# A ring of ten tiles, an inversion spread over 7.3 chains, back steps two chains later, and every fourth message pair split in halves

## The chip, the cores and the metric

One Trainium2 chip, one core, one launch. The metric is the device time of the kernel in microseconds (us), the median of some runs. The engines are TensorE (PE; PEld is its weight load), VectorE (DVE), ScalarE (ACT), GpSimd (POOL) and SyncE (SP, which here issues DMAs only). Each runs its own instructions in order, and semaphores tie them together.

## The reference, cut to what matters

The kernel computes two layers of a graph network on 2048 tokens of width 512. The change touches two of its stages.

The first is the gated delta recurrence of the first layer. Every token goes to 2 of 4 experts, so there are 4096 slots; the kernel works on them as 32 tiles of 128 slots, 8 heads of 64.

```python
def step(S, x):
    qt, kt, vt, bt, gt = x
    S = S * jnp.exp(gt)[..., None, None]
    kv = jnp.einsum('bhk,ebhkv->ebhv', kt, S)
    delta = (vt[None] - kv) * bt[..., None]
    S = S + kt[None, :, :, :, None] * delta[..., None, :]
    ot = jnp.einsum('bhk,ebhkv->ebhv', qt * scale, S)
    return (S, ot)
```

The second is the message passing of the second layer, over 32768 edges:

```python
msg = jax.nn.relu(x[src] + edge_attr @ W_e + b_e)
aggr = jax.ops.segment_sum(msg, dst, num_segments=x.shape[0])
```

## The kernel before, in words

Each stage is written as a `plan`, a list of (time, what, number) that is sorted by time. Every engine walks the list and issues what is its own, so the plan's times fix the order on each engine and nothing else; semaphores do the waiting. The unit of the plan's times is one chain in the recurrence and one pair of edge blocks in the message stage.

**The recurrence (tiles named `delta_...`).** A tile's 8 heads are worked in two chains of four heads, so there are NC = 64 chains. A chain has a front, which needs no state: GpSimd's mask (L1931) and ScalarE's part of it, transposes of q and k (L2068, copied by ScalarE), the decay sums on TensorE (L2080 to L2082, the last two in fp32r, one pass), their exp, GpSimd's weighting (L1936), the gram matmuls (L2093), and on VectorE the key products `BA` (L2194). `BA` and the transposed `kq` stand in a ring of R = 9 tiles; one part of `kq` lies in `X`.

The recurrence inside a tile asks for the inverse of a unit triangular matrix of 128 x 128 per head. Its diagonal blocks of 32 x 32 are inverted on VectorE for a batch of four tiles (eight chains) at once: SP writes the blocks to memory ("B out"), loads them as `Bs` with one block per partition ("B in", L1868), VectorE sets `Us` to minus `Bs` times a strict mask, with ones on the diagonal ("blocks set", L2169 and L2172), and walks 30 columns, each a product into `tmp` (L2176) and an update of `Us` (L2179). ScalarE copies the transpose to `Ls` (L1957), SP writes both out (L1871, L1873) and loads them in another layout for each tile ("UL in", L1883 and L1887). The rest of the inversion is small matmuls: Z (L2101, L2103), U (L2111 to L2115), Zb and T (L2043, L2050).

A chain's back carries the state: "through" (L2129), then on VectorE `r` and the first half of `o` (L2202, L2209), "solve" (L2138), `w` on ScalarE, "sums" (L2146 and L2151), then `state` (L2219) and `o` (L2225) on VectorE, and SP stores `o`. `kd` is GpSimd's weighted key (L1945). MAIN = 17.2 is the plan's distance from a chain's front to its back, MID = 15.8 that to Z; a batch's columns stand 5.4 chains wide in the plan behind 8 (q + 1) + 0.75 (3.0 chains wide for the first batch). With the backs run the products of a gate ("gate"), for which the stage's last chains have room.

**The message stage (tiles named `conv_...`).** The edges are sorted by target; 144 pairs of blocks of 128 edges are worked. Per pair: GpSimd gathers two blocks of source rows (L2702), TensorE transposes the attributes (L2717) and multiplies them by `W_e` into two banks (L2722), VectorE adds the gathered rows (L2768), ScalarE applies relu in place (L2749), TensorE sums by target with a one-hot matrix `hot` (L2730), and VectorE adds the bank to the accumulator (L2779). VectorE makes `hot` by comparison (L2760), for two pairs at a time. All of it is f32.

The planned times of the columns before are these:

```python
at = 0.75 + (5.4 if q else 3.0) * (31 - k) / 31
part = at - int(at)
part = part + 0.5 if part < 0.18 else 0.76 + 0.66 * (part - 0.18)
plan.append((first + int(at) + part, "block column", (q, k)))
```

## Time and profile before

| | us |
|---|---|
| median of 3 runs | 3208.61 (3206.28 to 3215.51) |
| the profiled execution, its own time | 3215.7 |
| its span | 3213.9 |
| TensorE busy | 2905.2 (90%) |
| VectorE busy | 1669.4 (52%) |
| GpSimd busy | 1488.0 (46%) |
| ScalarE busy | 1136.8 (35%) |
| mean granted clock of TensorE | 0.959 of full speed |

The busy shares are means over some twenty stages with different limits. What a stage is worth is read from windows of the trace that hold that stage alone: the recurrence lies at 1343 to 1948 us, the message stage at 2330 to 2777 us.

### The profile page before, as it was taken

The page shows a single profiled execution, that of the slowest core. Times are in us where ns is not written, and L with a number is a line of the kernel's source. Part 1 is how long each engine was busy: PE and PEld are TensorE (multiplying, and loading weights), DVE is VectorE, ACT ScalarE, POOL GpSimd, SP SyncE. Part 2 cuts the span into 40 slices and gives each one's busy share as a digit, 9 for nine tenths or more (in the row PEclk, how much of TensorE's full clock was granted, in tenths as well). Part 3 has the DMA queues.
Part 4 walks back from the last instruction along what each step waited for, and adds up shares of the span by engine and source line. Part 5 has one row for each costly group of instructions (what it writes and reads, how often), then busy time and mean ns, then how long its engine had stood idle before and what let it go on. Part 6 is the DMA issues. An engine that isn't in the chain of part 4 may idle for free.

```text
span 3213.9 us, 46196 instructions
## 1 busy us (share of the span) xinstructions
PE 2905.2 (90%) x16081; PEld 1658.6 (52%) x16081; DVE 1669.4 (52%) x3820; ACT 1136.8 (35%) x2501; POOL 1488.0 (46%) x1471
## 2 busy tenths in 40 slices
PE   6999999988899899858989898999999999999828
PEld 3433566667676644447777664444533333444424
DVE  7633355578344432268777643442267777521361
ACT  3312422289122222346666441220044444331201
POOL 0565756488654537633333204545566666200004
PEclk9999999999999999979999998999999999999959
DMA  5400001120111234434454454211176666500404
GB/s 173 140 19 5 7 25 49 46 71 16 32 52 44 72 121 165 166 104 126 117 143 128 136 148 159 77 53 38 49 227 199 198 205 190 156 0 27 183 0 132
DMA packets 275961, 321.38 MB, mean 100 GB/s; under 512 B 155807, under 2 KB 193569, under 8 KB 275732
## 3 DMA queue, kind: packets, MB, share of 16 engines
q1 hardware_dynamic: 219684, 182.57, 18.7%
q0 software_dynamic: 51840, 134.60, 13.4%
q8 instruction: 132, 2.16, 0.3%
q10 hardware_dynamic: 4208, 1.25, 0.2%
...
## 4 chain that ended last, share of the span: by engine, by line
PE 74%; issue 10%; DVE 5%; ACT 4%; POOL 4%; DMA 2%; SPq 0%; ACTq 0%; POOLq 0%; DVEq 0%
PE bank L2730 8%; PE bank L1522 5%; PE bank L2722 5%; PE bank L708 4%; PE bank L1301 4%; PE bank L2393 3%; PE bank L2884 3%; PE bank L2877 3%; PE bank L439 3%; PE bank L731 2%; PE bank L762 2%; PE bank L1117 2%; PE bank L2373 2%; PE bank L1311 2%; PE bank L858 2%
## 5 line engine op out<-in xcount | busy, mean ns | idle before, releaser
L2702 POOL DMA_INDIRECT conv_src<-xn_rows,keep x288 | 272.9, 948 | 175.7 <-DVE conv_msg L2768 110.4
L291 POOL DMA_INDIRECT sorted_bias<-perf_rec,place x256 | 259.7, 1014 | 146.0 <-PE bank L708 91.6
L2730 PE MATMUL bank<-conv_msg,conv_hot 128*128 128x512 f32 x576 | 273.0, 596 | 0.6 <-ACT conv_msg L2749 0.6
L2768 DVE TENSOR_TENSOR conv_msg<-bank,conv_src 128x512 f32<-128x512 f32 x288 | 185.5, 686 | 47.2 <-PE bank L2722 47.2
L1936 POOL TENSOR_TENSOR delta_dec<-delta_dec,rates_of 128x512 f32<-128x512 f32 x64 | 68.8, 1075 | 282.5 <-ACT delta_dec L1988 282.5
L666 POOL DMA_INDIRECT sorted_edge<-rec,place x128 | 127.1, 993 | 141.4 <-PE bank L1362 75.0
L2749 ACT ACTIVATE conv_msg<-conv_msg 128x1024 f32<-128x1024 f32 x144 | 152.0, 1056 | 102.0 <-DVE conv_msg L2768 102.0
L1117 PE MATMUL bank<-bias_prod,bias_hot 128*128 128x256 f32 x640 | 148.2, 387 | 25.1 <-ACT bias_hot L1070 13.0
L2722 PE MATMUL bank<-conv_we,conv_eT 64*128 64x512 f32 x576 | 164.5, 648 | 0.7 <-ACT conv_eT L2746 0.7
L1101 POOL TENSOR_TENSOR bias_prod<-bias_col,bias_rec 128x512 f32<-128x512 f32 x128 | 147.2, 1179 | 16.4 <-PE bank L1117 15.7
L1117 PEld LDWEIGHTS bank<-bias_prod,bias_hot 128*128 128x128 f32 x640 | 120.1, 192 | 53.7 <-issue 28.1
L2730 PEld LDWEIGHTS bank<-conv_msg,conv_hot 128*128 128x128 f32 x576 | 106.7, 205 | 71.5 <-issue 69.4
L2779 DVE TENSOR_TENSOR acc<-acc,bank 128x512 f32 x144 | 99.0, 688 | 72.6 <-PE bank L2730 72.6
L2194 DVE TENSOR_TENSOR delta_BA<-bank,delta_dec 128x512 f32<-128x512 f32 x128 | 82.1, 682 | 99.8 <-issue 51.3
L439 PE MATMUL bank<-xnT,perf_w 128*128 128x512 f32 x256 | 117.0, 600 | 3.5 <-ACT xnT L470 2.1
L3048 POOL TENSOR_TENSOR mlp_mv<-mlp_mv,neg_half 128x1 f32<-128x1 f32 x12 | 6.6, 552 | 242.3 <-DVE mlp_mv L3015 242.3
L889 ACT ACTIVATE mix_ex<-bank,mix_t 128x266 f32<-128x266 f32 x128 | 54.8, 479 | 159.9 <-DVE mix_t L947 159.9
L2884 PE MATMUL bank<-mlp_h,keep 128*128 128x512 f32 x256 | 110.5, 592 | 0.0
L2877 PE MATMUL bank<-mlp_hT,mlp_w 128*128 128x512 f32 x256 | 110.4, 592 | 0.0
L1079 ACT ACTIVATE bias_far<-C,bias_rec 128x128 f32<-128x128 f32 x320 | 102.2, 390 | 20.9 <-DMA bias_rec<-sorted_bias 14.2
L2138 PE MATMUL bank<-delta_r,delta_U 128*128 128x128 f32 (+1 forms) x512 | 71.7, 286 | 38.6 <-DVE delta_o L2209 32.1
L2722 PEld LDWEIGHTS bank<-conv_we,conv_eT 64*128 64x128 f32 x576 | 43.8, 186 | 109.7 <-issue 108.4
...
## 6 DMA issues: line engine op xcount, KB each, us to landing
...
conv_src<-xn_rows,keep POOLq DMA_INDIRECT x288, 3.6
...
sorted_bias<-perf_rec,place POOLq DMA_INDIRECT x256
```

Of the source, the lines that this page charges most:

```text
L291: POOL.indirect_dma_start(out=sorted_bias, out_offset=bass.IndirectOffsetOnAxis(ap=place[:, 0, c:c + 1], axis=0), in_=rec0[:, c, :], in_of ...
L439: a = PE.matmul(bank[i % 2], w[:, side, c, m * P:(m + 1) * P], xnT[:, c, nb * 512:(nb + 1) * 512], start=c == 0, stop=c == KC - 1)
L1101: engine.tensor_tensor(prod[:, q:q + 2, :, :], col[:, g % 2, k:k + 2, :].unsqueeze(2).broadcast_to([P, 2, H, GW]), rec[:, g % 3, k:k + 2, ...
L1117: a = PE.matmul(bank[u % 8][:, 0:W], hot[:, i // PER % 2, i % PER + j, :], prod[:, i % 8 + j, :, :].rearrange("p h j -> p (h j)"), start=j ...
L1522: a = PE.matmul(bank[3 + n % BANKS], xnT[:, c, t * P:(t + 1) * P], wts[k][:, c, :], start=c == 0, stop=c == KC - 1)
L2702: POOL.indirect_dma_start(out=src[:, n % 4, j, :], out_offset=None, in_=xn_rows, in_offset=bass.IndirectOffsetOnAxis(ap=rec[:, g % 3, k + ...
L2722: a = PE.matmul(bank[2 + 2 * q + j][:, :], eT[half, q, :], we[half, :], start=True, stop=True)
L2730: a = PE.matmul(bank[n % 2][:, :], hot[:, g % 2, k + j, :], msg[:, q, j, :], start=j == 0, stop=j == 1)
L2749: ACT.activation(msg[:, q, :, :], msg[:, q, :, :], AF.Relu).then_inc(*active.up())
L2768: DVE.tensor_tensor(msg[:, q, j, :], bank[2 + 2 * q + j][:, :], src[:, n % 4, j, :], ALU.add).then_inc(*raw.up())
L2877: a = PE.matmul(bank[i % 4], w1[:, c, m * P:(m + 1) * P], hT[:, c, columns(nb)], start=c == 0, stop=c == KC - 1)
L2884: return PE.matmul(bank[4 + nb], w2[:, c, m * P:(m + 1) * P], h1[:, c, columns(nb)], start=c == 0, stop=c == 2 * KC - 1)
```

## The change

In the recurrence the ring `BA` and `kq` have ten tiles instead of nine, and all steps of the backs and the middle of the inversion stand two chains later in the plan. To make room, `kd`, `r` and `w` have one copy instead of two, `o` three instead of four and `kv` two instead of three, with the waits that this asks for. The strict mask is left out of the set. The columns of a batch stand over 7.3 chains instead of 5.4 (from the second batch on), and a column is two entries of the plan: a product and an update; where a product falls ahead of the key products, its update stands behind them.

In the message stage every pair n with n % 4 == 1 is split: ScalarE writes relu of the message as `high` in fp32r, VectorE computes relu of the message less `high` as `low` in fp32r, and the scatter takes four fp32r matmuls instead of two f32 ones. `hot` is written as fp32r (its values are 0 and 1) and read as f32 by the other pairs. The two additions of gathered rows become one of double length, and the steps ahead of the sum stand up to 0.75 of a pair's time earlier.

```diff
...
-            R = 9
+            R = 10
             BT = 4
             NBT = ST // BT
             NC = 2 * ST
-            MID, MAIN = 15.8, 17.2
-            ALONE, TWO, FIRST = 16, 14, 16
+            MID, MAIN = 17.8, 19.2
+            ALONE, TWO, FIRST = 18, 16, 18
...
-            kv = sb("kv", [P, 3, 2, D])
+            kv = sb("kv", [P, 2, 2, D])
...
-            kd, r_, w = (sb(n, [P, 2, HG, HD]) for n in ("kd", "r", "w"))
-            o = sb("o", [P, 4, HG, HD])
+            kd, r_, w = (sb(n, [P, HG, HD]) for n in ("kd", "r", "w"))
+            o = sb("o", [P, 3, HG, HD])
...
-                plan.append((2 * t + (14.6 if t >= 2 else 13.6 + 0.4 * t), "UL in", t))
-                plan.append((2 * t + MAIN - 3.0, "load kv", t))
+                plan.append((2 * t + (16.6 if t >= 2 else 13.6 + 0.4 * t), "UL in", t))
+                plan.append((2 * t + MAIN - 2.6, "load kv", t))
...
-                    at = 0.75 + (5.4 if q else 3.0) * (31 - k) / 31
+                    at = 0.75 + (7.3 if q else 3.0) * (31 - k) / 31
                     part = at - int(at)
                     part = part + 0.5 if part < 0.18 else 0.76 + 0.66 * (part - 0.18)
-                    plan.append((first + int(at) + part, "block column", (q, k)))
-                plan.append((first + (6.33 if q else 5.19), "L copy", q))
-                plan.append((first + (6.34 if q else 5.2), "blocks out", q))
+                    plan.append((first + int(at) + part, "block product", (q, k)))
+                    plan.append((first + int(at) + (0.745 if q and part < 0.7 else part), "block update", (q, k)))
+                plan.append((first + (8.23 if q else 5.19), "L copy", q))
+                plan.append((first + (8.24 if q else 5.2), "blocks out", q))
...
                     if what == "load kv":
-                        if n >= 3:
-                            SP.wait_ge(*kd_ready.at(2 * (n - 3) + 2))
-                            SP.wait_ge(*r_ready.at(2 * (n - 3) + 2))
-                        SP.dma_start(kv[:, n % 3, :, :], slot_qkv[n * P:(n + 1) * P, D:3 * D].rearrange("p (a d) -> p a d", a=2)
-                                     ).then_inc(*kv_in[n % 3].up(16))
+                        if n >= 2:
+                            SP.wait_ge(*kd_ready.at(2 * (n - 2) + 2))
+                            SP.wait_ge(*r_ready.at(2 * (n - 2) + 2))
+                        SP.dma_start(kv[:, n % 2, :, :], slot_qkv[n * P:(n + 1) * P, D:3 * D].rearrange("p (a d) -> p a d", a=2)
+                                     ).then_inc(*kv_in[n % 2].up(16))
...
+                        if n >= 1:
+                            POOL.wait_ge(*state_sum.at(n))
+                        POOL.tensor_tensor(kd[:, :, :], kv[:, t % 2, 0, g * W:(g + 1) * W].rearrange("p (h d) -> p h d", d=HD),
                                            mid(bg[:, t, hs], HD), ALU.mult).then_inc(*kd_ready.up())
...
                     if what == "w":
                         ACT.wait_ge(*solved.at(n + 1))
-                        ACT.activation(flat4(w[:, n % 2, :, :]), MA[:, 256:512], AF.Copy, scale=-1.0).then_inc(*w_ready.up())
+                        if n >= 1:
+                            ACT.wait_ge(*attended.at(n))
+                        ACT.activation(flat4(w[:, :, :]), MA[:, 256:512], AF.Copy, scale=-1.0).then_inc(*w_ready.up())
...
                     if what == "blocks set":
                         DVE.wait_ge(*bs_in.at(16 * (n + 1)))
-                        if n == 0:
-                            DVE.wait_ge(*strict_in.at(16))
                         if n >= 1:
                             DVE.wait_ge(*u_out.at(16 * n))
                             DVE.wait_ge(*L_ready.at(n))
-                        DVE.scalar_tensor_tensor(flat(Us), flat(Bs), -1.0, strict[:, :], ALU.mult, ALU.mult
-                                                 ).then_inc(*blocks.up())
+                        DVE.tensor_scalar(flat(Us), flat(Bs), -1.0, None, ALU.mult).then_inc(*blocks.up())
                         DVE.wait_ge(*blocks.now())
                         DVE.memset(flat(Us)[:, 0:32 * 32:33], 1.0).then_inc(*blocks.up())
-                    if what == "block column":
+                    if what == "block product":
                         q, k = n
                         DVE.wait_ge(*blocks.now())
                         DVE.tensor_tensor(tmp[:, 0:k, k + 1:32], Bs[:, 0:k, k:k + 1].broadcast_to([P, k, 31 - k]),
                                           Us[:, k:k + 1, k + 1:32].broadcast_to([P, k, 31 - k]), ALU.mult).then_inc(*blocks.up())
+                    if what == "block update":
+                        q, k = n
                         DVE.wait_ge(*blocks.now())
                         a = DVE.tensor_tensor(Us[:, 0:k, k + 1:32], Us[:, 0:k, k + 1:32], tmp[:, 0:k, k + 1:32], ALU.subtract)
                         if k > 1:
...
                     if what == "r":
                         DVE.wait_ge(*through.at(n + 1))
-                        DVE.wait_ge(*kv_in[t % 3].at(16 * (t // 3 + 1)))
+                        DVE.wait_ge(*kv_in[t % 2].at(16 * (t // 2 + 1)))
+                        if n >= 1:
+                            DVE.wait_ge(*solved.at(n))
                         for i, h in enumerate(heads):
-                            a = DVE.scalar_tensor_tensor(r_[:, n % 2, i, :], (MA, MB)[i % 2][:, (i // 2) * HD:(i // 2 + 1) * HD],
-                                                         eg[:, 0, t, h:h + 1], kv[:, t % 3, 1, h * HD:(h + 1) * HD],
+                            a = DVE.scalar_tensor_tensor(r_[:, i, :], (MA, MB)[i % 2][:, (i // 2) * HD:(i // 2 + 1) * HD],
+                                                         eg[:, 0, t, h:h + 1], kv[:, t % 2, 1, h * HD:(h + 1) * HD],
                                                          ALU.mult, ALU.subtract)
                         a.then_inc(*r_ready.up())
-                        if n >= 4:
-                            DVE.wait_ge(*o_out[n % 4].at(16 * (n // 4)))
+                        if n >= 3:
+                            DVE.wait_ge(*o_out[n % 3].at(16 * (n // 3)))
...
-            hot = sb("hot", [P, 2, PER, P])
+            hot = sb("hot", [P, 2, PER, P], F32H)
...
+            high, low = (sb(n, [P, 2, 2, D], F32H) for n in ("high", "low"))
...
+
+            def in_halves(n):
+
+                return n % 4 == 1
 
             plan = []
             for n in range(EG):
-                for what, at in (("gather", -3.6), ("turn", -2.3), ("eT", -2.2), ("edge", -1.75), ("raw", -1.4), ("relu", -0.85),
+                for what, at in (("gather", -3.9), ("turn", -3.05), ("eT", -2.9), ("edge", -2.15), ("raw", -1.8), ("relu", -1.25),
                                  ("sum", 0.0), ("add", 0.6)):
                     plan.append((n + at, what, n))
+                if in_halves(n):
+                    plan.append((n - 0.7, "low", n))
                 if n % 2 == 0:
                     plan.append((n - 2.2, "hot", n // 2))
...
                         PE.wait_ge(*prepared.at(2 * n // SOME + 1))
                         if n >= 2:
                             PE.wait_ge(*added.at(n - 1))
+                        if not in_halves(n):
+                            for j in range(2):
+                                a = PE.matmul(bank[n % 2][:, :], hot[:, g % 2, k + j, :].bitcast(F32), msg[:, q, j, :],
+                                              start=j == 0, stop=j == 1)
+                            a.then_inc(*summed.up())
+                            continue
                         for j in range(2):
-                            a = PE.matmul(bank[n % 2][:, :], hot[:, g % 2, k + j, :], msg[:, q, j, :], start=j == 0, stop=j == 1)
+                            PE.matmul(bank[n % 2][:, :], hot[:, g % 2, k + j, :], high[:, n // 4 % 2, j, :], start=j == 0, stop=False)
+                        PE.wait_ge(*lowered.at(n // 4 + 1))
+                        for j in range(2):
+                            a = PE.matmul(bank[n % 2][:, :], hot[:, g % 2, k + j, :], low[:, n // 4 % 2, j, :], start=False,
+                                          stop=j == 1)
                         a.then_inc(*summed.up())
...
                     if what == "relu":
-                        ACT.wait_ge(*raw.at(2 * n + 2))
-                        ACT.activation(msg[:, q, :, :], msg[:, q, :, :], AF.Relu).then_inc(*active.up())
+                        ACT.wait_ge(*raw.at(n + 1))
+                        if not in_halves(n):
+                            ACT.activation(msg[:, q, :, :], msg[:, q, :, :], AF.Relu).then_inc(*active.up())
+                            continue
+                        if n >= 8:
+                            ACT.wait_ge(*summed.at(n - 7))
+                        ACT.activation(high[:, n // 4 % 2, :, :], msg[:, q, :, :], AF.Relu).then_inc(*active.up())
...
-                        for j in range(2):
-                            DVE.tensor_tensor(msg[:, q, j, :], bank[2 + 2 * q + j][:, :], src[:, n % 4, j, :],
-                                              ALU.add).then_inc(*raw.up())
+                        DVE.tensor_tensor(msg[:, q, :, :], pairs[1 + q][:, :, :], src[:, n % 4, :, :], ALU.add).then_inc(*raw.up())
+                    if what == "low":
+                        DVE.wait_ge(*active.at(n + 1))
+                        if n >= 8:
+                            DVE.wait_ge(*summed.at(n - 7))
+                        DVE.scalar_tensor_tensor(low[:, n // 4 % 2, :, :], msg[:, q, :, :], 0.0, high[:, n // 4 % 2, :, :].bitcast(F32),
+                                                 ALU.max, ALU.subtract).then_inc(*lowered.up())
```

**VectorE in the recurrence, one chain in the middle of a batch.** First before, then the change (`delta_tmp` rows are products, `delta_Us` rows updates, `delta_BA` the key products).

```order
L2202 SCALAR_TENSOR_TENSOR delta_r<-bank,delta_eg,delta_kv 128x64 x4
L2209 TENSOR_TENSOR delta_o<-bank,delta_eg 128x2x64 x2
L2176 TENSOR_TENSOR delta_tmp<-delta_Bs,delta_Us 128x18x13
L2179 TENSOR_TENSOR delta_Us<-delta_Us,delta_tmp 128x18x13
L2194 TENSOR_TENSOR delta_BA<-bank,delta_dec 128x2x256 x2
L2176 TENSOR_TENSOR delta_tmp<-delta_Bs,delta_Us 128x17x14
L2179 TENSOR_TENSOR delta_Us<-delta_Us,delta_tmp 128x17x14
L2176 TENSOR_TENSOR delta_tmp<-delta_Bs,delta_Us 128x16x15
L2179 TENSOR_TENSOR delta_Us<-delta_Us,delta_tmp 128x16x15
L2219 SCALAR_TENSOR_TENSOR delta_state<-delta_state,delta_ep,bank 128x64 x2
L2176 TENSOR_TENSOR delta_tmp<-delta_Bs,delta_Us 128x15x16
L2179 TENSOR_TENSOR delta_Us<-delta_Us,delta_tmp 128x15x16
```

```order
L2202 SCALAR_TENSOR_TENSOR delta_r<-bank,delta_eg,delta_kv 128x64 x4
L2209 TENSOR_TENSOR delta_o<-bank,delta_eg 128x2x64 x2
L2172 TENSOR_TENSOR delta_tmp<-delta_Bs,delta_Us 128x21x10
L2192 TENSOR_TENSOR delta_BA<-bank,delta_dec 128x2x256 x2
L2177 TENSOR_TENSOR delta_Us<-delta_Us,delta_tmp 128x21x10
L2172 TENSOR_TENSOR delta_tmp<-delta_Bs,delta_Us 128x20x11
L2177 TENSOR_TENSOR delta_Us<-delta_Us,delta_tmp 128x20x11
L2219 SCALAR_TENSOR_TENSOR delta_state<-delta_state,delta_ep,bank 128x64 x2
L2172 TENSOR_TENSOR delta_tmp<-delta_Bs,delta_Us 128x19x12
L2177 TENSOR_TENSOR delta_Us<-delta_Us,delta_tmp 128x19x12
L2225 TENSOR_TENSOR delta_o<-delta_o,bank 128x256
```

Between the first half of `o` and the state there were three pairs of product and update, one of them ahead of the key products; now there are two, and of the first only the product stands ahead of the key products.

**SP in the recurrence, from the end of one batch's inversion to the load of the next.** First before, then the change.

```order
L1871 DMA sol_u<-delta_Us 128x1024
L1873 DMA sol_l<-delta_Ls 128x1024
L1883 DMA delta_U<-sol_u 32x8x32 x4
L1887 DMA delta_Lf<-sol_l 32x8x32 x3
L1850 DMA keep<-slot_qkv 128x1024
L1910 DMA slot_out<-delta_o 128x256
L1862 DMA sol_b<-delta_BA 32x8x32 x4
L1910 DMA slot_out<-delta_o 128x256
L1856 DMA delta_kv<-slot_qkv 128x1024
L1868 DMA delta_Bs<-sol_b 128x1024
```

```order
L1868 DMA sol_u<-delta_Us 128x1024
L1870 DMA sol_l<-delta_Ls 128x1024
L1865 DMA delta_Bs<-sol_b 128x1024
L1880 DMA delta_U<-sol_u 32x8x32 x4
L1884 DMA delta_Lf<-sol_l 32x8x32 x3
```

The load of `Bs` stood behind two stores and a batch of "B out"; now it is the next DMA after the writes of the finished batch, since these have moved two chains later and it has not.

**TensorE in the message stage, two pairs of which the first is a split one.** First before, then the change.

```order
L2730 MATMUL bank<-conv_msg,conv_hot 128x512 x2
L2722 MATMUL bank<-conv_we,conv_eT 128x512 x2
L2717 MATMUL bank<-C,conv_att 128x128
L2730 MATMUL bank<-conv_msg,conv_hot 128x512 x2
L2722 MATMUL bank<-conv_we,conv_eT 128x512 x2
L2717 MATMUL bank<-C,conv_att 128x128
```

```order
L2742 MATMUL bank<-conv_high,conv_hot 128x512 x2
L2745 MATMUL bank<-conv_low,conv_hot 128x512 x2
L2728 MATMUL bank<-conv_we,conv_eT 128x512 x2
L2723 MATMUL bank<-C,conv_att 128x128
L2737 MATMUL bank<-conv_msg,conv_hot 128x512 x2
L2728 MATMUL bank<-conv_we,conv_eT 128x512 x2
L2723 MATMUL bank<-C,conv_att 128x128
```

The two f32 matmuls of the split pair have become two with `high` and two with `low`; the rest of the pair stands where it stood.

## Rows read from the trace of the kernel before

**Rows 1.** Windows of four stages: us, busy time of each engine, PEclk, DMA share, GB/s.
```profile
1343.00:1437.00 94.00, 56.92 (x386) 38.19 (x386) 50.82 (x107) 45.28 (x118) 37.34 (x36) 0.80 0.32 95
1437.00:1812.00 375.00, 339.71 (x5114) 280.11 (x5114) 285.61 (x874) 238.29 (x650) 124.27 (x138) 0.97 0.47 126
1812.00:1948.00 136.00, 120.86 (x1658) 90.41 (x1657) 58.58 (x220) 47.49 (x140) 11.39 (x18) 0.91 0.49 143
2330.00:2777.00 447.00, 441.75 (x1296) 151.49 (x1296) 326.97 (x503) 207.37 (x306) 272.93 (x288) 0.99 0.67 197
```

**Rows 2.** Chain of waits, message stage: start, us, what, count.
```profile
2399.57 1.72 PE bank L2730 x4
...
2402.61 1.72 PE bank L2730 x4
```

**Rows 3.** Timeline of TensorE, recurrence, a decay sum.
```profile
1562.54 0.59 PE L2081 MATMUL bank<-delta_dec_half,delta_after_half 128*128 128x512 f32 x1
1562.97 0.40 PE L2082 MATMUL bank<-delta_dec_half,delta_after_half 128*128 128x512 f32 x1
```

**Rows 4.** VectorE groups of the message stage: count, busy us, mean ns, idle before.
```profile
L2768 DVE TENSOR_TENSOR conv_msg<-bank,conv_src 128x512 f32<-128x512 f32 x288 | 185.5, 686 | 47.2 <-PE bank L2722 47.2
L2779 DVE TENSOR_TENSOR acc<-acc,bank 128x512 f32 x143 | 98.3, 688 | 70.8 <-PE bank L2730 70.8
```

**Rows 5.** Timelines of GpSimd and of VectorE, message stage.
```profile
2506.70 0.95 POOL L2702 DMA_INDIRECT conv_src<-xn_rows,keep  x1 [0.30 <-issue]
...
2506.89 0.68 DVE L2760 TENSOR_TENSOR conv_hot<-C,keep 128x512 f32<-128x512 f32 x1
```

**Rows 6.** Timeline of VectorE, recurrence, chains with inversion columns.
```profile
1504.78 0.41 DVE L2225 TENSOR_TENSOR delta_o<-delta_o,bank 128x256 f32<-128x256 f32 x1
...
1516.56 1.12 DVE L2179 TENSOR_TENSOR delta_Us<-delta_Us,delta_tmp 128x234 f32<-128x234 f32 x1
...
1521.80 0.41 DVE L2225 TENSOR_TENSOR delta_o<-delta_o,bank 128x256 f32<-128x256 f32 x1
```

**Rows 7.** Timeline of VectorE, chains without columns, then the next set.
```profile
1543.77 1.29 DVE L2194 TENSOR_TENSOR delta_BA<-bank,delta_dec 128x512 f32<-128x512 f32 x2 [2.74 <-issue]
...
1550.83 1.29 DVE L2194 TENSOR_TENSOR delta_BA<-bank,delta_dec 128x512 f32<-128x512 f32 x2 [2.99 <-issue]
...
1560.53 1.23 DVE L2169 SCALAR_TENSOR_TENSOR delta_Us<-delta_Bs,delta_strict 128x1024 f32<-128x1024 f32 x1 [0.40 <-DMA delta_Bs<-sol_b]
```

**Rows 8.** Waits, middle part of the recurrence: total, times, longest us.
```profile
PE bank L2138 <- DVE delta_o L2209: 31.5, 32, 2.0
```

**Rows 9.** Window of one batch of eight chains, columns as in rows 1.
```profile
1497.00:1560.00 63.00, 56.47 (x876) 46.36 (x876) 49.34 (x150) 40.43 (x111) 21.65 (x24) 1.00 0.50 133
```

**Rows 10.** VectorE groups, middle part, inversion columns.
```profile
L2179 DVE TENSOR_TENSOR delta_Us<-delta_Us,delta_tmp 128x58 f32<-128x58 f32 (+4 forms) x179 | 74.3, 415 | 6.1
L2176 DVE TENSOR_TENSOR delta_tmp<-delta_Bs,delta_Us 128x58 f32<-128x58 f32 (+4 forms) x179 | 68.5, 382 | 2.4
```

**Rows 11.** Timeline of SP's DMA queue, end of a batch and next load.
```profile
1539.89 0.32 SPq L1871 DMA_DIRECT2D sol_u<-delta_Us  x1
1542.11 0.32 SPq L1873 DMA_DIRECT2D sol_l<-delta_Ls  x1
...
1555.80 0.32 SPq L1868 DMA_DIRECT2D delta_Bs<-sol_b  x1
```

**Rows 12.** Timeline of TensorE, lead-in, fronts alone.
```profile
1356.79 0.38 PE L2080 MATMUL bank<-delta_mask_bits 128*128 128x512 bf16 x1 [0.88 <-issue]
...
1360.00 0.38 PE L2080 MATMUL bank<-delta_mask_bits 128*128 128x512 bf16 x1 [0.88 <-issue]
```

**Rows 13.** Timeline of VectorE, tail, one row per chain.
```profile
1923.86 0.42 DVE L2225 TENSOR_TENSOR delta_o<-delta_o,bank 128x256 f32<-128x256 f32 x1 [0.55 <-PE bank L2151]
...
1947.01 0.42 DVE L2225 TENSOR_TENSOR delta_o<-delta_o,bank 128x256 f32<-128x256 f32 x1 [1.42 <-PE bank L2151]
```

**Rows 14.** Window of the last chains, columns as in rows 1.
```profile
1925.00:1948.00 23.00, 18.73 (x201) 16.56 (x200) 6.44 (x27) 5.07 (x15) 0.61 (x1) 0.70 0.33 99
```

35 lines of the change are left out of this document (14 added, 21 removed).

## The prediction

> **What bounds the kernel now.** I read the stage windows first [rows 1], to see how much of each stage TensorE is busy; then, inside the two stages that the diff touches, the chain of waits, the grouped instructions and the timelines.
>
> In the message stage TensorE is busy 442 of 447 us and every other engine has room (VectorE 327, GpSimd 273) [rows 1]. The chain of waits there is TensorE alone, and it repeats every 2402.61 - 2399.57 = 3.04 us, one pair of edge blocks; 1.72 of them are the scatter matmuls [rows 2]. What is taken from these comes off the span.
>
> The recurrence has three parts: fronts alone (94 us), both together (375 us), backs alone (136 us) [rows 1]. In the middle part a chain (half a tile) without inversion columns takes 1550.83 - 1543.77 = 7.1 us, and VectorE waits 2.7 and 3.0 us in it before its key products: TensorE sets the pace [rows 7]. With columns, two chains take 1521.80 - 1504.78 = 17.0, 8.5 each [rows 6], and over the middle part TensorE stands 31.5 us in 32 waits before the solve because VectorE has not finished r and the first half of o [rows 8]. So some 5.4 chains of every 8 go at VectorE's pace and the rest at TensorE's.
>
> **The change, part by part.**
>
> Message stage. Every fourth pair, 36 of 144, replaces two f32 scatter matmuls by four in fp32r (high and low part of the message). The trace has fp32r matmuls of 128x512 in the decay sums: L2081 ends at 1562.54 + 0.59 = 1563.13, L2082 at 1562.97 + 0.40 = 1563.37, so one takes 0.24 us, its weight load included [rows 3]. Four take 0.96 against 1.72: 0.76 x 36 = 27 us off the chain. Bounds: 31 if each is an even quarter of the f32 matmul that it stands for (1.72/8 = 0.215), 18 if every third halved pair loses its gain to a wait.
>
> Is there a new wait? Four pairs will take TensorE 4 x 3.04 - 0.76 = 11.4 us. VectorE has in them eight message additions (or four of double length, at most 8 x 0.69), four scatter additions (0.69) [rows 4], two comparisons (0.68) [rows 5] and now one subtraction on 128x1024; the nearest row, the set in the recurrence, took 1.23 us [rows 7]: 10.9 us at most. The subtraction stands 0.7 of a pair's time ahead of the matmuls that need it, and the high part's matmuls go first. GpSimd issues two gathers per pair, each 0.95 us and 0.30 between them [rows 5]: 10.0 of 11.4 us. ScalarE only writes its result elsewhere. I take no wait; the cover is thin (0.5 us on VectorE), and each microsecond that it falls short in four pairs costs 36 us.
>
> A lock between VectorE and GpSimd would speak against this. In the trace a comparison with two inputs in SBUF ran from 2506.89 to 2507.57 while a gather was issued, and both kept their usual 0.68 and 0.95 us [rows 5]. The Trainium skill ("SBUF — State Buffer", the section on a bandwidth-pool intuition that is wrong) says that while VectorE runs an operation over both ports GpSimd cannot write the descriptors of its own DMAs. By that rule the new subtraction would add its length to GpSimd's queue, which would then need 11.2 of 11.4 us and still not be the bound.
>
> Inversion over 7.3 chains. VectorE is busy 49.3 of the 63 us of a batch of eight chains [rows 9]. Its work for the chains themselves: in the middle part 285.6 us [rows 1], less 74.3 + 68.5 for columns [rows 10] and five sets of 1.23 [rows 7], leaves 137 us over 46 chains, 3.0 each. A batch's inversion is then 49.3 - 8 x 3.0 = 25 us. Over 5.4 chains that is 4.7 + 3.0 = 7.7 us a chain, above TensorE's 7.1; over 7.3 chains it is 3.5 + 3.0 = 6.5, below it. Measured against load, the slow chains took (63 - 2.6 x 7.1)/5.4 = 8.25 for 7.7, 7% more; 6.5 with that is 7.0. At best the batch falls to 8 x 7.1 = 56.8, 6.2 us less. But the peak is thicker than the mean: an update takes 1.12 us instead of 0.42 when a GpSimd operation runs beside it [rows 6, 10]. From below I take a quarter of the best, 1.5 us. I take 4, two thirds of the best, because the order still puts one or two pairs ahead of r. The update that is held back until after the key products changes no work; it lets TensorE's next gram matmuls start some 0.4 us sooner, inside the 4.
>
> The set of the next batch. Its mask falls away: 1.23 us [rows 7] becomes a scaling with one input. No row has this form at this size; it lies between the 1.23 and the 0.68 of a 128x512 operation [rows 5], and I take 0.9, 0.3 less. Against it, there is now one chain, not three, between the last column and the set. SP must write U, wait for ScalarE's copy, write L (2.2 us after U), then load Bs; that load took 1560.53 - 1555.80 = 4.7 us [rows 7, 11]. That is 7.3 us for a chain of 7.1, where the wait was 0.4 [rows 7]: 0 to 1.5 us more, also inside the 4.
>
> The ring of ten and the two chains' delay. No work is added or removed: two chains leave the middle part, and two fronts and two backs run alone. The middle part is now 375/46 = 8.15 us a chain; then 44 x (8.15 - 0.5) = 337, so -38 us. Lead-in: a front alone takes 1360.00 - 1356.79 = 3.2 us [rows 12], so +6.4 at most; r of the first chain no longer stands behind the second batch's set, so 3 at least; I take +5. Tail: its last three backs took 1947.01 - 1923.86 = 23.2, 7.7 us each [rows 13], at a mean granted clock of 0.70, between the levels 1.2 and 2.4 GHz [rows 14]; two more cost 15 (14 at 7.1, 17 at 8.5). Sum: -38 + 5 + 15 = -18 us.
>
> The single copies of kd, r and w, three of o and two of kv add waits on work that ends most of a chain earlier (the sums, solve or attention of the chain before; for kv 2.3 chains, against a load the size of Bs's 4.7 us), so nothing. Behind SP's wait for r before it loads kv stand the store of o and the loads of U and L, whose slack is 1.1 chains.
>
> Sum: -27 - 18 = -45 us. The profiled execution took 3215.7 us about a span of 3213.9, 7 above the median of 3208.6. From the median: **3164 us**; its profile nearer 3171.
>
> **The rivals.**
> 1. The chains gain little: VectorE's waits move to the set, one after each batch, and the columns before r still keep the solve waiting. For it: the gap of 7.1 us against 7.3. Against it: a load of 6.5 us. At 1.5 us a batch the middle part gives -16 - 8 = -24, the recurrence -4, the kernel -31: 3178.
> 2. The message stage stops being TensorE's, VectorE being late with the low part or the additions. For it: 10.9 of 11.4 us; against it: that is an upper bound. Half the gain goes: -13 - 18 = -31: 3178.
> 3. The whole excess goes (56.8 a batch): 44 x 0.78 = 34, with -16 and +20 it is -30; the kernel -57: 3152.
> 4. Slower: the tables come too late. U is written at once after the last column, L 2.2 us later [rows 11], then both are read back in small loads; the first Z of a batch stands 1.5 chains, 10.8 us, behind the last column, and stood 1.4 behind it. If each of seven batches waited there for x us, the kernel would be slower from 7x > 45, x > 6.4. At 8 us: 3220. Against it: the distance grew.
> 5. TensorE's clock is granted less: it is 0.97 in the middle part, 0.80 in the lead-in [rows 1], 0.70 at the end [rows 14]. Two more thin chains at each end at the lower level cost +10 to +20 beyond the sum; with rival 1, about 3195.
> On the last, the Trainium skill ("TensorE: Matmul & The Clock Gate", Part 1) says that the clock is low by default and that activity releases it; the trace agrees, with 0.99 in its fullest stage and less at the thin ends. By the rule the longer ends stay partly at the lower level, which is case 5.
>
> **How the numbers follow.** The sum as argued 0.60; rival 1 0.15; rival 2 0.08; rival 3 0.08; rival 4 0.04; rival 5 0.05. The range takes in rivals 1 to 3 with the bounds of the matmul: 3147 (rival 3 with 31 for the messages, and a microsecond) to 3187 (rival 1 with 18 for the messages). A measurement here tells 0.3%, 10 us, from no change. Faster 0.91 (the first four cases), same 0.05, slower 0.04.
>
> **What the profile will show.** Message stage: four fp32r matmuls within 1.0 us, four pairs in 11.4 us, the stage some 27 us shorter, no wait of TensorE for the low part. Recurrence: chains with columns 7.3 to 7.6 us instead of 8.5, TensorE's wait before the solve far under 31.5 us, 0 to 2 us of wait at each set, the first solve 3 to 6 us later after the first decay, a tail near 151 us. Wrong would be: chains that stay above 8 us, sets that wait over 3 us, Z waiting for the L load in each batch, or gathers longer than 0.95 us beside the subtraction.

## The result, and the profile after

The changed kernel took 3185.97 us (median of 5 runs, 3181.11 to 3194.41) against 3208.82 (5 runs, 3206.28 to 3215.51) of the kernel before, taken together: ratio 0.9929, interval 0.9911 to 0.9947, 22.8 us faster. The forecast was 45 faster, 3164; the range held the time, at its upper end. The same kernel was measured twice more (below): 0.9967 (0.9951 to 0.9982) on a chip where before took 3253 us, and 0.9904 (0.9886 to 0.9921) on one where it took 3212.

The profiled execution had a span of 3179.3 us, its own time 3181.1, the fastest of its five; that of before was the slowest of its five. The difference of the two profiles, 34.6 us, is therefore more than the medians give.

Windows of the changed kernel, the stages of [rows 1] at their new places, then one batch of eight chains [rows 9]; columns as there:

```profile
1343.00:1450.00 107.00, 65.65 (x436) 45.03 (x438) 57.33 (x128) 50.02 (x131) 40.73 (x41) 0.78 0.32 90
1450.00:1788.00 338.00, 314.60 (x4876) 257.32 (x4874) 253.14 (x828) 226.23 (x620) 114.40 (x132) 1.00 0.48 131
1788.00:1930.00 142.00, 127.48 (x1855) 97.43 (x1853) 63.28 (x245) 54.55 (x157) 12.65 (x20) 0.95 0.52 152
2313.00:2742.00 429.00, 414.54 (x1296) 151.76 (x1296) 346.20 (x396) 209.28 (x306) 290.45 (x288) 0.99 0.70 205
1492.00:1553.60 61.60, 57.34 (x892) 46.86 (x892) 45.49 (x150) 41.37 (x114) 21.00 (x24) 1.00 0.50 134
```

Two things stand out beside [rows 1]. In the message stage TensorE is now 14 us short of always busy, where it lacked 5. And the middle of the recurrence has clock 1.00, where it had 0.97.

**Message stage: a wait nobody had before.** Chain of waits of the changed kernel in this stage (start, us, what):

```profile
2455.45 0.02 ACT conv_msg L2766
...
2456.42 1.05 ACT conv_att L2756
2457.47 0.04 issue
2457.51 0.33 PE bank L2723
2457.84 0.47 PE bank L2742 x2
2458.32 0.46 PE bank L2745 x2
2458.78 1.06 PE bank L2728 x4
2459.84 0.26 PE bank L2723
2460.10 1.72 PE bank L2737 x4
```

The four fp32r matmuls (L2742, L2745) take 0.47 + 0.46 = 0.93 us where 1.72 stood, as forecast. But once in eight pairs the chain leaves TensorE and runs over ScalarE's pack, the copy of the next eight pairs of edge rows into `att` (L2756, 1.05 us). Timeline of ScalarE and TensorE at another such place (in brackets the idle time before, and who ended it):

```profile
2408.75 1.06 ACT L2766 ACTIVATE conv_msg<-conv_msg 128x1024 f32<-128x1024 f32 x1 [0.96 <-DVE conv_msg L2788]
...
2409.71 1.04 ACT L2756 ACTIVATE conv_att<-keep 128x1024 f32<-128x1024 f32 x1
2410.80 0.14 PEld L2723 LDWEIGHTS bank<-C,conv_att 128*128 128x128 f32 x1 [1.38 <-ACT conv_att L2756]
2410.81 0.33 PE L2723 MATMUL bank<-C,conv_att 128*128 128x128 f32 x1 [0.55 <-ACT conv_att L2756]
```

The plan has the pack at n - 3.0, as before, while the change moved the turn that reads it from n - 2.3 to n - 3.05. The pack, queued behind a relu, now ends after the turn is due. From one turn to the next it is 3.04 us for an ordinary pair, 2.25 for a split one and 3.66 at these places; from the first turn to the last 417.4 us against 435.9 before.

**Recurrence: three terms, two of them off.** From the timelines, the first output of a chain (L2225) came at 1441.1 before and 1453.7 after, the last decay sum at 1810.5 and 1786.6, the last output at 1947.0 and 1929.3 (the changed kernel's times are put 0.14 us later, so that the first decay sums, 1343.21 and 1343.07, meet). So the lead-in is +12.6 us (forecast +5), the middle 369.4 to 332.9, -36.5 (-38), the tail 136.5 to 142.7, +6.2 (+15). Their sum is -17.7 for -18, which is chance: the lead-in lost what the tail saved, and part of the middle's gain is not what I had argued.

VectorE of the changed kernel in the middle, two chains with columns:

```profile
1563.98 0.30 DVE L2172 TENSOR_TENSOR delta_tmp<-delta_Bs,delta_Us 128x150 f32<-128x150 f32 x1
1565.95 1.29 DVE L2192 TENSOR_TENSOR delta_BA<-bank,delta_dec 128x512 f32<-128x512 f32 x2 [1.68 <-issue]
1567.16 0.44 DVE L2177 TENSOR_TENSOR delta_Us<-delta_Us,delta_tmp 128x150 f32<-128x150 f32 x1
...
1570.41 0.85 DVE L2202 SCALAR_TENSOR_TENSOR delta_r<-bank,delta_eg,delta_kv 128x64 f32<-128x64 f32 x4
...
1573.23 1.29 DVE L2192 TENSOR_TENSOR delta_BA<-bank,delta_dec 128x512 f32<-128x512 f32 x2 [1.28 <-issue]
```

From key products to key products it is 7.3 us here, from output to output 7.1 to 8.4 over a batch, where a chain with columns took 8.5 [rows 6]; the batch is 61.6 us for 63.2 to 63.8. VectorE idles 1.3 to 1.7 us ahead of the key products and then has no gap until r; the held-back update stands in that full stretch. TensorE's wait for VectorE before the solve fell to half [rows 8], not to nearly nothing, and the set waits little. The second row is new, a wait for ScalarE (below):

```profile
PE bank L2137 <- DVE delta_o L2209: 15.5, 26, 1.4
PE bank L2137 <- ACT delta_U L2002: 7.1, 5, 1.4
```

```profile
1554.24 0.69 DVE L2166 TENSOR_SCALAR delta_Us<-delta_Bs 128x1024 f32<-128x1024 f32 x1 [0.84 <-DMA delta_Bs<-sol_b]
```

**Recurrence: another wait nobody had before.** Once in each batch, at the first solve behind the end of the columns, TensorE stands 1.4 us for ScalarE's copy of the finished inverse (`U`, L2005 before, L2002 after). ScalarE before, then ScalarE and TensorE of the changed kernel:

```profile
1539.80 0.38 ACT L2005 ACTIVATE delta_U<-bank 64x256 f32<-64x256 f32 x1
1540.08 2.00 ACT L1957 ACTIVATE delta_Ls<-delta_Us 128x1024 f32<-128x1024 f32 x1
```

```profile
1546.77 1.98 ACT L1954 ACTIVATE delta_Ls<-delta_Us 128x1024 f32<-128x1024 f32 x1
1548.78 0.38 ACT L1999 ACTIVATE delta_Zb<-bank 64x256 f32<-64x256 f32 x1
1549.18 0.38 ACT L2002 ACTIVATE delta_U<-bank 64x256 f32<-64x256 f32 x1
1549.61 1.10 PE L2137 MATMUL bank<-delta_r,delta_U 128*128 128x128 f32 x8 [1.44 <-ACT delta_U L2002]
```

The 2 us copy of the transpose (`L copy`) stood behind the two small copies (Zb and T) and now stands ahead of them. In the plan those two lie at 0.25 and 0.26 of a chain's time; the change moved the L copy from 6.33 to 8.23 behind a batch's start, from just behind them to just ahead. In the four profiles with the spread of 5.4 the L copy stands behind the small ones, in the ten with 7.3 ahead of them; all ten have this wait, five times each, and none of the four has it in the middle. VectorE's r and first half of `o` were done at 1547.5 and TensorE's last decay sum at 1548.2, so the solve could have started 1.4 us sooner. No run moved the L copy back; that it would give up to 1.4 us a batch, 7 us in five, is an estimate from these rows.

In the lead-in VectorE of the changed kernel stands at the second batch's set, and the key products of chain 17 are queued behind it; TensorE then idles for those key products, ahead of its next gram matmuls:

```profile
1424.30 1.29 DVE L2192 TENSOR_TENSOR delta_BA<-bank,delta_dec 128x512 f32<-128x512 f32 x2 [1.93 <-POOL delta_dec L1933]
1431.84 0.69 DVE L2166 TENSOR_SCALAR delta_Us<-delta_Bs 128x1024 f32<-128x1024 f32 x1 [6.25 <-DMA delta_Bs<-sol_b]
...
1433.12 1.28 DVE L2192 TENSOR_TENSOR delta_BA<-bank,delta_dec 128x512 f32<-128x512 f32 x2
```

```profile
1434.55 2.08 PE L2092 MATMUL bank<-delta_more_kq 64*128 64x256 f32 x8 [3.78 <-DVE delta_BA L2192]
```

### The profile page after: what moved, and what is told of

Same layout as the page of the kernel before. It is cut to its first block, busy times and chain, and to the rows that moved or that the text cites. A ratio compares the mean times of both kernels' runs of the same rounds, so it can differ in the third digit from the quotient of the medians.

```text
span 3179.3 us, 46211 instructions
## 1 busy us (share of the span) xinstructions
PE 2868.6 (90%) x16081; PEld 1650.9 (52%) x16081; DVE 1667.8 (52%) x3712; ACT 1138.0 (36%) x2501; POOL 1497.0 (47%) x1471
## 4 chain that ended last, share of the span: by engine, by line
PE 80%; DVE 7%; ACT 6%; issue 5%; DMA 2%; POOL 1%; SPq 0%; DVEq 0%; ACTq 0%; POOLq 0%
PE bank L1522 5%; PE bank L2737 5%; PE bank L708 4%; PE bank L2728 4%; PE bank L1301 4%; PE bank L2393 3%; PE bank L2909 3%; PE bank L2902 3%; PE bank L439 3%; PE bank L2137 2%; PE bank L731 2%; PE bank L2150 2%; PE bank L762 2%; PE bank L1117 2%; PE bank L2128 2%
## 5 line engine op out<-in xcount | busy, mean ns | idle before, releaser
L2708 POOL DMA_INDIRECT conv_src<-xn_rows,keep x288 | 290.4, 1009 | 140.8 <-issue 95.9
L2737 PE MATMUL bank<-conv_msg,conv_hot 128*128 128x512 f32 x432 | 203.5, 594 | 0.0
L2788 DVE TENSOR_TENSOR conv_msg<-bank,conv_src 128x1024 f32<-128x1024 f32 x144 | 175.7, 1220 | 18.0 <-PE bank L2728 18.0
L2766 ACT ACTIVATE conv_msg<-conv_msg 128x1024 f32<-128x1024 f32 x108 | 114.2, 1057 | 87.3 <-DVE conv_msg L2788 87.3
L2909 PE MATMUL bank<-mlp_h,keep 128*128 128x512 f32 x256 | 110.5, 592 | 0.0
L2737 PEld LDWEIGHTS bank<-conv_msg,conv_hot 128*128 128x128 f32 x432 | 80.1, 205 | 52.4 <-issue 51.8
L1942 POOL TENSOR_TENSOR delta_kd<-delta_kv,delta_bg 128x256 f32<-128x256 f32 x64 | 39.2, 613 | 130.4 <-PE bank L2145 129.9
```

The lines of the kernel that those rows point to most:

```text
L2708: POOL.indirect_dma_start(out=src[:, n % 4, j, :], out_offset=None, in_=xn_rows, in_offset=bass.IndirectOffsetOnAxis(ap=rec[:, g % 3, k + ...
L2737: a = PE.matmul(bank[n % 2][:, :], hot[:, g % 2, k + j, :].bitcast(F32), msg[:, q, j, :], start=j == 0, stop=j == 1)
L2788: DVE.tensor_tensor(msg[:, q, :, :], pairs[1 + q][:, :, :], src[:, n % 4, :, :], ALU.add).then_inc(*raw.up())
L2909: return PE.matmul(bank[4 + nb], w2[:, c, m * P:(m + 1) * P], h1[:, c, columns(nb)], start=c == 0, stop=c == 2 * KC - 1)
```

## The experiments

Each time stands beside runs of the kernel before on the same chip. The two halves, the early pack and the update at once shared a chip (before 3214.0 us); the second measurement of the change, the spread of 5.4, the earlier load and the two pairs another (3253.2); all four together, every second pair split and 5.4 with the update at once a third (3212.7); the third measurement of the change stood on a fourth (3211.7). The microseconds faster or slower are worked out from the ratio; the difference of the two medians lies up to 3 us beside them.

**The two halves apart.** The kernel before with the changed message stage, and the changed kernel with the old message stage.

> The kernel before, with the change's message stage and with its recurrence left as it was. In the changed kernel's profile the turns of the message stage take 417.4 us from first to last against 435.9 before. Theory (the stage gives its 18 us wherever it stands): ratio near 0.994, 17 to 20 us faster than before; the pattern 3.04 us for a pair, 2.25 for a split one and 3.66 for one in each eight is found again. Rival (the message stage gave its forecast 27 us, and the recurrence then gave nothing or cost in the median): 25 to 29 us faster, ratio 0.991 to 0.992.

Measured: 3195.92 us, ratio 0.9949 (0.9933 to 0.9965), 16.4 us faster; turns 417.4 us from first to last, the same pattern. The stage gives what its own profile shows.

> The changed kernel with the message stage of before. Its profile ended the recurrence 17.7 us sooner than the profile of before, but that execution of before was its slowest, with dips of the granted clock in the recurrence that cost it about 10 us. Theory (the recurrence itself gives only some 5 to 8 us, and the dips made the rest): 3 to 9 us faster than before in the median, ratio 0.997 to 0.999. Rival (the profiles' 17.7 us are the recurrence's): ratio near 0.9945.

Measured: 3200.35 us, 0.9962 (0.9944 to 0.9981), 12.2 us faster: between the two theories, with an interval (6 to 18) that reaches both. Its profile has the changed kernel's batches of 61.6 us to a few hundredths. 16.4 + 12.2 = 28.6.

The third measurement of the whole change was to say whether the halves add.

> The changed kernel a third time. Its first measurement gave 22.8 us less than before, the second, on a chip where the kernel of before took 3253 us, 10.7 less; the two halves of the change measured apart gave 16.4 and 12.2, 28.6 in all. Theory (the halves add): 25 to 31 us faster than before on a chip where before takes 3205 to 3215 us. Rival (together they give less than apart): 18 to 23 us.

Measured: 3183.50 us, 0.9904, 30.8 us faster. That the halves add fits this, within the 6 us either way that its interval leaves; the first 22.8 and this 30.8 are two measurements of one kernel, so differences of 8 us between kernels on different chips say little.

**The pack.** One number:

```diff
-                    plan.append((n - 3.0, "pack", n // HALF))
+                    plan.append((n - 3.5, "pack", n // HALF))
```

> The changed kernel with ScalarE's packing of the next eight pairs of edge rows half a pair sooner in the order (n - 3.5 in place of n - 3.0), so that it no longer stands right ahead of the copy that frees the turn, and behind a relu. Theory (the one long period in each eight pairs, 3.66 us for 3.04, is the turn waiting for the pack): the long periods go, 17 times 0.62 us, 9 to 11 us faster than the changed kernel, 32 to 34 faster than before (ratio 0.9895 to 0.990). Rival 1 (the stage is near VectorE's 10.9 us in 11.4 for four pairs and takes the freed time as waits for the raw sums or the low parts): 2 to 6 us. Rival 2 (the pack then delays a relu by its 1.05 us and moves the wait to the sums): 0 us.

Measured: 3174.09 us, 0.9875 (0.9858 to 0.9892), 40.2 us faster than before. Beside the changed kernel's 22.8 and 30.8 that is 9 to 17 more; the stage itself is exact, 407.4 us from first turn to last for 417.4. Its timeline:

```profile
2405.83 1.05 ACT L2756 ACTIVATE conv_att<-keep 128x1024 f32<-128x1024 f32 x1
2406.90 1.06 ACT L2766 ACTIVATE conv_msg<-conv_msg 128x1024 f32<-128x1024 f32 x1
...
2408.33 0.33 PE L2723 MATMUL bank<-C,conv_att 128*128 128x128 f32 x1
```

The turn has no wait, eight pairs take 22.73 us, and 435.9 - 407.4 = 28.5 us is the forecast's 27 with the one wait removed. Both rivals fall.

**How far the split goes.** Also with the early pack, every second pair split (`return n % 2 == 1`, the halves' buffers and waits to match).

> The changed kernel with the pack half a pair sooner and every second pair split in halves instead of every fourth. By the rows of the changed kernel four pairs then cost PE 2 x 3.04 + 2 x 2.25 = 10.6 us, and VectorE 4 x (1.22 merged sum + 0.69 addition + 0.34 hot) + 2 x 1.22 low = 11.4 us, before waits. Theory (at every fourth pair VectorE was just under PE, the next one passes it): 11.4 to 12 us for four pairs, no faster than the 11.36 with every fourth pair split, 0 to 20 us slower than the kernel with the pack alone moved. Rival (VectorE's sums overlap and PE stays the bound): 10.6 us for four pairs, stage 27 us shorter.

Measured: 3195.28 us, 0.9945 (0.9924 to 0.9966); 425.4 us from first turn to last, 11.9 for four pairs against 11.4, though undisturbed stretches of eight pairs took 21.2, the rival's 10.6 for four. So it is slower, as the theory said, but not by the mechanism it named. VectorE's work is 310 of 350 us, and TensorE waits 25.8 of them for the low part; the engine that is full is GpSimd. Groups of GpSimd in 350 us (2350 to 2700) of before, of the changed kernel, with the early pack, and with every second pair split (count, busy us, mean ns, idle before):

```profile
L2702 POOL DMA_INDIRECT conv_src<-xn_rows,keep x231 | 218.9, 947 | 132.3 <-DVE conv_msg L2768 92.8 <-issue 39.4
```

```profile
L2708 POOL DMA_INDIRECT conv_src<-xn_rows,keep x241 | 242.7, 1007 | 108.6 <-issue 68.5 <-DVE conv_msg L2788 40.1
```

```profile
L2708 POOL DMA_INDIRECT conv_src<-xn_rows,keep x247 | 275.5, 1116 | 76.2 <-issue 69.5 <-DVE conv_msg L2788 6.7
```

```profile
L2708 POOL DMA_INDIRECT conv_src<-xn_rows,keep x235 | 277.1, 1179 | 73.6 <-issue 69.3 <-DVE conv_msg L2788 4.2
```

With its fixed 0.30 us between gathers (235 x 0.30 = 70 us) it is busy 347 of 350 us, and 2 x (1.18 + 0.30) = 2.96 us a pair is 11.8 of the 11.9 us for four. A gather grows when one of VectorE's operations with both inputs in SBUF, the subtraction or the comparison, runs beside it. In the 350 us with the early pack the 153 gathers beside neither took 0.94 to 0.96 us, the 62 beside a comparison alone 1.19 in the mean and the 31 beside a subtraction 1.78. In the kernel with every second pair split:

```profile
2490.05 1.21 DVE L2793 SCALAR_TENSOR_TENSOR conv_low<-conv_msg,conv_high 128x1024 fp32r<-128x1024 f32 x1
2490.12 1.96 POOL L2708 DMA_INDIRECT conv_src<-xn_rows,keep  x1 [0.30 <-issue]
```

1.96 us for 0.95: 1.01 more, beside 1.14 us of the subtraction. The Trainium skill ("SBUF — State Buffer", the section on the bandwidth-pool intuition) tells of such a wait of GpSimd, which cannot write its descriptors until VectorE lets go of the shared port, but for a `tensor_copy`, with one input; the trace has it for operations with two inputs. By these sums it decides here how far the split can go: with the early pack GpSimd is as full (275.5 + 247 x 0.30 = 350 us), and TensorE too. Shares between a fourth and a half of the pairs, and an order that keeps VectorE's two operations off the gathers, were not tried.

**The inversion's spread and the held-back update.**

```diff
-                    plan.append((first + int(at) + (0.745 if q and part < 0.7 else part), "block update", (q, k)))
+                    plan.append((first + int(at) + part, "block update", (q, k)))
```

> The changed kernel with each key-product block's update right behind its product again, not held back to 0.745 of its chain; the spread over 7.3 chains stays. The profile shows VectorE idle 1.2 to 1.9 us ahead of the key products in each chain with columns, while the held update (0.44 to 0.70 us) stands behind them and ahead of the right side r. Theory (the held order costs in the middle of the recurrence): 30 to 40 chains by 0.3 to 0.5 us, 9 to 20 us faster than the changed kernel. Rival (without the hold the pair stands between the state and the key products, on VectorE's other tight path, as in the kernel before): equal or 5 to 15 us slower.

Measured: 3182.77 us, 0.9906 (0.9891 to 0.9921). A batch took 60.7 to 61.1 us for 61.6, so holding the updates back cost, but 0.8 us a batch where I expected 1.5 to 3; by the last decay sum it was 4 us ahead of the changed kernel, counted from the first one, and the tail (147.7 us for 142.7, its last 30 us at clock 0.78 for 1.00) gave that back. The time is not told apart from the changed kernel's.

Next, the spread alone undone, with and without the hold (`5.4 if q` for `7.3 if q`, the copy of L and the writes at their old 6.33 and 6.34).

> The changed kernel with the inversion of a batch spread over 5.4 chains as before (L copy and blocks out back at 6.33 and 6.34), all else of the change kept: ring of ten, back steps two chains later, set with one operand, updates held back. Theory (the spread is what shortens a batch, and the other parts are even): a batch of eight goes back from 61.6 to 63.5 to 64 us, six batches, 10 to 13 us slower than the changed kernel. Rival (the lighter set and the ring give the gain, the spread nothing): 61 to 62 us a batch, within 3 us of the changed kernel.

Measured: 3276.55 us, 1.0078 (1.0050 to 1.0106) where the unaltered changed kernel on the same chip had 0.9967: 36 us slower than it, three times the theory's price. Its batches took 64.8 to 67.8 us; of the 39 us between the two profiles 30 lie in the recurrence behind its first output. It says that the change depends on the spread, not what the spread alone is worth, since the clock fell in every batch (below).

> The changed kernel with the inversion spread over 5.4 chains and each update right behind its product: of the recurrence's change only the ring of ten, the back steps two chains later and the one-operand set are left. With the updates held back and 5.4 chains an undisturbed batch of eight took 64.8 us, before 63.5 to 63.8. Theory (the held updates made the 1.3 us, and ring, set and later back steps are even in the middle): 63.2 to 64.2 us where the clock stays up. Rival (the later back steps themselves lengthen the chains): 64.5 us or more. Both expect falls of the granted clock again, of 2 to 4 us each, in the stretches where VectorE is busy without a gap and PE waits.

Measured: 3198.09 us, 0.9956 (0.9940 to 0.9973). Of the five batches from the first output on, four took 63.2 to 63.4 us and one 66.2, with a fall of the clock. So ring, later back steps and light set are even in the middle, as forecast, and the 14 us that this kernel is faster than before are no more than the message stage's 16.4. With updates at once, 7.3 chains for 5.4 are worth 63.4 - 60.8 = 2.6 us a batch, the new wait for ScalarE (1.4 us, only with 7.3) already paid, and holding back takes 0.8 of them again. With 5.4 chains it does more harm: TensorE's longest wait for the solve is 3.4 us, where it is 1.9 with updates at once.

**The clock is the rest.** Windows of the kernel before around its longest wait for the solve (columns as in rows 1), and that wait in TensorE's timeline, with another one a batch later:

```profile
1586.00:1588.00 2.00, 0.47 (x3) 0.04 (x1) 1.93 (x8) 0.60 (x1) 0.81 (x1) 1.00 0.60 182
1590.00:1598.00 8.00, 8.00 (x95) 6.98 (x95) 7.26 (x24) 4.10 (x13) 0.00 (x0) 0.50 0.50 114
```

```profile
1588.47 1.22 PE L2138 MATMUL bank<-delta_r,delta_U 128*128 128x128 f32 x8 [2.00 <-DVE delta_o L2209]
...
1682.55 0.21 PE L2101 MATMUL bank<-delta_Lf,delta_BA 32*32 32x32 f32 x1 [1.61 <-DMA delta_Lf<-sol_l]
```

TensorE stood 2.00 us behind VectorE, and 1.61 for the load of L, and then, from about 1 and 2 us later, ran for some 10 and 7 us at 0.50 of the clock, 1.2 GHz for 2.4: those two batches took 67.2 and 67.8 us, the others 63.2 to 63.8. The message-alone kernel, whose recurrence is the old one, has two such batches (67.2 and 67.6), behind waits of 1.90 and 1.28 us, and one with a fall of some 3 us behind a wait of 1.88 that took 63.7 like the rest. Not every such wait is followed by a fall, so its length alone does not decide it. With spread 5.4 and the updates held back the wait is longer and every batch has a fall; its wait, and the window of its first batch:

```profile
1626.96 1.08 PE L2137 MATMUL bank<-delta_r,delta_U 128*128 128x128 f32 x8 [3.43 <-DVE delta_o L2209]
```

```profile
1490.34:1557.33 66.99, 61.80 (x892) 51.47 (x891) 46.14 (x151) 41.77 (x114) 21.53 (x24) 0.92 0.47 126
```

No profile with the spread of 7.3, ten of them, has a long batch among its first five: TensorE's waits there are 1.4 us at most in the changed kernel. From the first output the five batches took 325.7 us before and 308.2 after: of the 17.5, 9.7 are 1.9 a batch and 7.8 are what the two batches with a fall took longer.

**Starting the second batch sooner.**

```diff
-                plan.append((first + 0.3, "B in", q))
+                plan.append((first + (-0.1 if q == 1 else 0.3), "B in", q))
```

> The changed kernel as it stands, run beside the next three on the same chip, so that they and the earlier experiments can be set against it. Both theories: 20 to 30 us faster than before (it was 22.8 faster, 0.9929, in its own measurement), profile like the one shown.

> The changed kernel with the load of the second batch's blocks (Bs) on SyncE ahead of the seven loads of the inverse for t = 1, not behind them. In the changed kernel VectorE waits 6.25 us for it at the set (it starts at 1431.84), the key products of chain 17 stand behind the set, and the first output comes at 1453.7 against 1441.1 before. Theory (the order on SyncE makes 4.3 us of that wait): the set starts 4 us sooner, the first output 4 to 7 us sooner, and all after it, 4 to 7 us faster than the changed kernel. Rival (the first back step then waits for its inverse, which comes later): 0 to 2 us faster.

Measured on the same chip: changed kernel 3240.59 us, 0.9967; this one 3250.45, 0.9973 (0.9957 to 0.9989). No difference in time. In the profiles the set's wait is 4.17 us for 6.96 beside it (6.25 in the changed kernel's first profile), and from the decay sum of chain 16 to the first output it takes 29.4 us for 32.1. So SyncE's order is 2.7 us of the lead-in's excess, less than the 4 to 7 I expected. On this chip all kernels were slower, and in the message stage several engines stood at once for up to 5 us on nothing in the kernel, as here in the changed one:

```profile
2367.24 0.28 ACT L2762 ACTIVATE conv_eT<-bank 128x128 f32<-128x128 f32 x1 [4.91 <-remote]
```

That took 434.0 us instead of 417.4 for the stage and may be why the gain was only 10.7 us there; what stood behind it wasn't tried.

**Column pairs where VectorE idles.** Updates at once, and

```diff
-                    part = part + 0.5 if part < 0.18 else 0.76 + 0.66 * (part - 0.18)
+                    part = 0.5 + 0.4 * part if part < 0.5 else 0.76 + 1.08 * (part - 0.5)
```

> The changed kernel with updates right behind their products, as in the experiment on that, and with up to two column pairs of the inversion in each chain placed between the right side r and the key products (where VectorE is idle 1.2 to 1.7 us) instead of one product. Theory (from the key products to r VectorE works without a gap, so each pair taken out of that stretch shortens the chain): batches at 57.5 to 60 us against 60.8 with the updates at once and 61.6 in the changed kernel; 8 to 20 us faster than the changed kernel. Rival (PE's own order sets the chain once the update is gone): batches at 60.5 to 61, no more than the 0.8 us of the updates.

Measured: 3234.72 us, 0.9946 (0.9929 to 0.9964), the changed kernel beside it 0.9967. Batches 59.7 us, clock 1.00:

```profile
1544.00:1603.70 59.70, 56.52 (x884) 46.81 (x882) 48.87 (x149) 40.93 (x113) 21.71 (x24) 1.00 0.53 140
```

1.1 us a batch less than with the updates at once, so the place of the pairs matters as the theory said, at the low end of its gain. In time it is 7 us, and the intervals of the two kernels overlap.

**All four together**, with the set and first columns of the second batch also behind the key products of chain 17 (`1.73 if q == 1 else 1.05` for the set).

> The changed kernel with four orders mended: ScalarE's pack half a pair sooner; updates right behind their products; up to two column pairs between r and the key products; and at the start of the recurrence the load of the second batch's blocks ahead of the loads of the inverse, with the set and the first columns of that batch behind the key products of chain 17. From the profiles: message stage 407 us from first turn to last (10 less than the changed kernel), batches of eight 59.7 us against 61.6 (five of them, 9 less), and at the start 3 us from the load plus, by theory, 3 to 5 from the key products no longer behind the set. Theory: 20 to 27 us faster than the changed kernel, 42 to 50 faster than before where no stalls disturb it (ratio 0.985 to 0.987). Rival (start and tail give the batches' gain back, as the tail did with the updates at once): 30 to 40 faster than before.

Measured: 3158.67 us (3152.29 to 3160.58), 0.9824 (0.9800 to 0.9849): 56.5 us faster than before, 26 to 34 more than the change as it was. Message stage 408.3 us, batches 59.7, first output 103.3 us behind the first decay sum for 110.5. VectorE in the lead-in now does the key products first and the set after:

```profile
1427.27 1.29 DVE L2194 TENSOR_TENSOR delta_BA<-bank,delta_dec 128x512 f32<-128x512 f32 x2 [1.55 <-POOL delta_dec L1935]
1430.62 0.69 DVE L2168 TENSOR_SCALAR delta_Us<-delta_Bs 128x1024 f32<-128x1024 f32 x1 [2.07 <-DMA delta_Bs<-sol_b]
```

## Why the prediction was half right

**"I take no wait" (message stage, -27).** This is the step that failed. The matmuls' term was right (0.93 us for four, forecast 0.96), and the stage gives 28.5 us once the pack moves. I weighed VectorE and GpSimd and dismissed ScalarE with "only writes its result elsewhere": a fixed time in the plan, n - 3.0, against a turn that moved past it. 17 waits of 0.62 us are 10.5 us, and 18.5 were left. It was rival 2's size by another engine; rival 2 itself, VectorE late, falls with the early pack.

**GpSimd.** The lock is there, and gathers longer than 0.95 us beside the subtraction were one of the prediction's signs of being wrong: they rose from 0.95 to 1.01 us in the mean, 1.12 with the early pack. The 11.2 of 11.4 us that the prediction gave for GpSimd with the lock is what the early pack shows (11.3 of 11.4), and it wasn't the bound, as said. Its plain 10.0 us was 10.5 in the changed kernel. The row that spoke for it, a comparison beside a gather that kept its 0.95 us, was a rare one: before, 3 of 230 gathers had a comparison beside them.

**Batch of eight (-4).** Mis-sized: -1.9 where the clock stays up, and two chains of each batch still took 8.3 to 8.4 us, over the 8 us named as a sign of being wrong. ScalarE was left out here too: up to 1.4 of the missing 2.1 us are the wait behind the L copy. The spread gives 2.6 net of that wait; "the update that is held back ... lets TensorE's next gram matmuls start sooner" had the sign wrong, +0.8. Rival 1's mechanism, waits at the set, did not come: 1.5 us in two waits over the middle. Against that stand the clock's falls, which the prediction saw as 0.97 in the middle part and did not ask about: 7.8 us of the profiles' 36.5. Rival 4's wait, of Z for the load of L, was there before (1.61 us at 1682.55) and is gone, as the longer distance had it; the tables come late at the other end, at T's copy. In runs of the recurrence alone the whole is 12.2 us for the forecast's 18.

**The set.** 0.69 us, not 0.9, for a one-input operation on 128x1024: as long as a two-input one on half as many.

**Lead-in (+5).** Mis-sized, +12.6, and its set waited 6.25 us, over the 3 us named as a sign. I priced two fronts at 3.2 us and let r come out from behind the second set, but not that the fronts of chains 17 and on, which now run alone, themselves stand behind that set. The two orders mended there take back 7.2 us of it, 2.7 by the earlier load.

**Tail (+15).** Mis-sized for two reasons. The first is a wait of before that the sum did not see leaving: the last set stood 4.71 us for its load, with r of a chain behind it, TensorE at the same time 4.38 us for the gate's load, and 15.3 us passed between two outputs there (1820.12 to 1835.38). In the changed kernel that set waits 0.93 us, and no two outputs lie more than 10.0 apart.

```profile
1825.25 1.23 DVE L2169 SCALAR_TENSOR_TENSOR delta_Us<-delta_Bs,delta_strict 128x1024 f32<-128x1024 f32 x1 [4.71 <-DMA delta_Bs<-sol_b]
```

The second is the clock. I priced two backs at 7.7 us from rows at 0.70. The changed kernel's last chains took 6.0 at 1.00; in its third measurement 9 us at the lower level, in a tail of 153.5 us for 142.7:

```profile
1911.00:1930.00 19.00, 14.55 (x232) 12.88 (x230) 7.08 (x30) 5.18 (x16) 1.70 (x3) 1.00 0.37 123
```

```profile
1911.00:1941.00 30.00, 25.61 (x256) 23.08 (x256) 7.33 (x30) 5.71 (x18) 1.84 (x3) 0.55 0.23 72
```

So the 6.2 us between the two profiles is no measure of two backs. With the old recurrence the tails were 136.5 and 132.5 us; with the new one and its spread of 7.3, 142.3 to 153.5.

What stays open: how many falls of the clock an unprofiled run of the kernel before has, and so how the recurrence's 12.2 us divide between the spread and the clock; 5.4 of the 12.6 us of the lead-in; and what the L copy behind the two small ones would give.
